# A decoder layer with routed experts on one core: the list of expert units is made in routing's last tile, and first loads and constants move with it

## What is computed

```python
logits = x_flat.astype(jnp.float32) @ gate_weight.astype(jnp.float32).T
scores = jax.nn.sigmoid(logits)
...
_, topk_idx = jax.lax.top_k(tmp, K)                      # K = 8 of E = 64 experts
...
xe = jnp.zeros((E, CAP, H), x.dtype).at[sorted_e, pos].set(tok_sorted, mode='drop')
h = jax.nn.silu(jnp.einsum('ech,efh->ecf', xe, w1)) * jnp.einsum('ech,efh->ecf', xe, w3)
ye = jnp.einsum('ecf,ehf->ech', h, w2)
...
out = jax.ops.segment_sum(vals * flat_w[:, None], flat_t, num_segments=T)
shared = jax.nn.silu(x @ shared_gate.T) * (x @ shared_up.T) @ shared_down.T
return (out + shared).reshape(B, S, H)
```

## Time and profile before

| | us |
|---|---|
| median of the timed runs (3) | 3640.21 |
| lowest, highest | 3639.7, 3642.63 |
| time of the profiled execution | 3623.67 |
| its span | 3621.7 |
| TensorE busy in the span | 3162.4 (87%) |
| VectorE, ScalarE, GpSimd busy | 2182.0, 1384.8, 1553.3 |

### The profile page before, as it was taken

The page is one execution under the profiler, slowest core; times in us unless marked ns, Lnnn a source line. Parts: engine busy times, 40 slices in busy tenths (PEclk is TensorE's granted clock), DMA queues, the critical chain, the costliest instruction groups (busy, mean ns, idle before and its releaser), DMA issues. The chain is left out here.

```text
span 3621.7 us, 63739 instructions
## 1 busy us (share of the span) xinstructions
PE 3162.4 (87%) x18589; PEld 2035.1 (56%) x18589; DVE 2182.0 (60%) x4857; ACT 1384.8 (38%) x3155; POOL 1553.3 (43%) x1113
## 2 busy tenths in 40 slices
PE   7998989999899998989796999999788882999990
PEld 4444444454444444444344777776676671888880
DVE  3645556455564645556354788886566662777775
ACT  1443434434354443434322556664000001444441
POOL 3352434424244342434531333342366664666661
PEclk8999999989999999999898999998899996999995
DMA  4122121222203122120283112121321212898996
GB/s 120 40 68 72 33 69 39 68 72 53 78 14 87 48 68 72 31 58 18 86 271 116 58 62 68 62 62 47 106 58 52 60 51 85 232 254 252 248 254 208
DMA packets 189332, 343.99 MB, mean 95 GB/s; under 512 B 36153, under 2 KB 54714, under 8 KB 188090
## 3 DMA queue, kind: packets, MB, share of 16 engines
q1 hardware_dynamic: 132922, 242.51, 23.5%
q0 software_dynamic: 28800, 48.43, 5.9%
q10 hardware_dynamic: 27392, 50.34, 3.8%
HBM read 206.96 MB, written 83.89 MB: 80 GB/s over the span
## 5 line engine op out<-in xcount | busy, mean ns | idle before, releaser
L544 ACT ACTIVATE sa_probs<-sa_s 128x512 f32<-128x512 f32 (+3 forms) x1280 | 615.0, 537 | 747.5 <-PE sa_s L435 414.8
L329 POOL TENSOR_TENSOR sa_both<-sa_probs 128x2048 f32<-128x2048 f32 (+2 forms) x160 | 589.6, 3685 | 696.0 <-PE sa_pv L462 684.5
L401 PE MATMUL sa_w<-sa_parts 96*128 96x512 f32 (+3 forms) x1280 | 518.9, 457 | 115.6 <-DVE sa_pmax L603 34.8
L435 PE MATMUL sa_s<-sa_parts 128*128 128x512 f32 (+3 forms) x1280 | 459.7, 410 | 18.9 <-ACT sa_probs L544 13.7
L607 DVE TENSOR_REDUCE sa_pmax<-sa_w 128x1 f32<-128x512 f32 (+3 forms) x768 | 419.3, 584 | 87.7 <-PE sa_w L401 84.4
L401 PEld LDWEIGHTS sa_w<-sa_parts 96*128 96x128 f32 x1280 | 238.4, 197 | 408.0 <-issue 119.8
L603 DVE CUSTOM_DVE_ANT_0 sa_w<-sa_w,sa_maskS 128x512 f32<-128x512 f32 (+3 forms) x512 | 326.3, 649 | 230.9 <-PE sa_w L401 224.5
L435 PEld LDWEIGHTS sa_s<-sa_parts 128*128 128x128 f32 x1280 | 244.5, 195 | 130.5 <-ACT sa_probs L544 64.4
L1384 POOL DMA_INDIRECT token_and_weight_of_slot<-rt_entry,rt_sl x256 | 254.7, 995 | 142.5 <-issue 74.9
L453 PE MATMUL sa_pv<-sa_probs,sa_values 128*32 128x512 f32 (+3 forms) x2560 | 275.7, 549 | 0.0
L1202 ACT ACTIVATE xa_sm<-xa_sm,xa_nmax 128x154 f32<-128x154 f32 x512 | 208.8, 410 | 64.6 <-DVE xa_nmax L1146 64.6
(11 more groups left out here) (240 smaller groups left out, 5786.5 us busy)
## 6 DMA issues: line engine op xcount, KB each, us to landing
ex_w<-in_w SPq DMA_DIRECT2D x138, 512.0 KB
sa_parts<-sa_halves SPq DMA_DIRECT2D x384, 128.0 KB, 2.5
sa_xt<-in_xT SPq DMA_DIRECT2D x32, 1024.0 KB
scratch_attention_T<-sa_oT SPq DMA_DIRECT2D x32, 256.0 KB, 2.2
on_at<-scratch_attention_T SPq DMA_DIRECT2D x32, 256.0 KB, 3.3
on_xr<-in_x SPq DMA_DIRECT2D x32, 256.0 KB, 3.3
scratch_x<-on_xn ACTq DMA_DIRECT2D x32, 256.0 KB, 2.1
scratch_x_T<-on_xnT ACTq DMA_DIRECT2D x32, 256.0 KB, 3.3
```

The costliest lines, as they stand in the source:

```text
L329: pool.tensor_tensor(both[:, :, 0:w], probs[:, even, :, 0:w], probs[:, odd, :, 0:w], ALU.add).then_inc(both_ready, 1)
L401: nc.tensor.matmul(ps[:, 0:w], qparts[0:3 * HD, h, q0:q0 + P], kparts[0:3 * HD, h, k0:k0 + w], start=True, stop=True).then_inc(work_ready, 1)
L435: mm = nc.tensor.matmul(ps[:, 0:w], kparts[:, h, kb * P:(kb + 1) * P], qparts[:, h, q0:q0 + w], start=True, stop=not diag)
L544: nc.scalar.activation(probs[:, r % NPB, h, 0:w], sbank[n % NSB][:, 0:w], ACT.Exp).then_inc(exp_done, 1)
```

## The change

A class `Lists` holds what both stages use: the list, the table's copy in SBUF (`entries`), the matrix for transposes, a zero column, both buffers of the experts' weights, and the semaphores of their loads and of `added`. The second block of routing goes. Its parts and the experts' head are moved:

- GpSimd: the three constants of the list stand at routing's head, ahead of `consts`; behind it the experts' four constant steps and the four stores into `unused`.
- TensorE: the sum over `cum` behind the last tile, into `gps` (with two waits that are met by then).
- VectorE: `list_units` in the last tile's `locate`, behind the reciprocal and ahead of the wait for GpSimd's product.
- SyncE, behind its last tile: the list goes from SBUF to SBUF instead of by DRAM; it reads the first unit and loads its weights; then it waits for all scatters and loads the table. The first load in `experts` is gone.
- `experts` has no wait for constants any more; its loop is the same.

```diff
@@ route_and_shared
+                sp.wait_ge(worklist_done, 1)
+                sp.wait_ge(lists.set_up, 1)
+                sp.dma_start(lists.worklist[0:1, 0:2 * UNITS].rearrange("o (u c) -> o u c", c=2), wli[:]).then_inc(lists.worklist_in, 16)
+                sp.wait_ge(lists.worklist_in, 16)
+                first = sp.value_load(lists.worklist[0:1, 0:1], min_val=0, max_val=UNITS - 1) // UPE
+                lists.load_weights(sp, first, 0)
+                for s in range(2):
+                    sp.wait_ge(scat[s], 128 * (NT // 2))
+                sp.dma_start(lists.entries[:].rearrange("p n e c -> p n (e c)"),
+                             table.rearrange("(n p e) c -> p n (e c)", p=P, e=E_)).then_inc(lists.entries_in, 16)
...
+                step(pool.iota(iou[:], pattern=[[1, UNITS]], base=0, channel_multiplier=0))
+                step(pool.iota(row[:], pattern=[[0, 1]], base=1, channel_multiplier=1))
+                step(pool.memset(zrow[:], 0.0))
                 pool.sem_inc(consts, 1)
+                step(pool.memset(lists.worklist[:], 0))
+                step(pool.memset(lists.zero[:], 0.0))
+                step(pool.memset(lists.identf[:], 0.0))
+                step(pool.affine_select(out=lists.identf[:], in_=lists.identf[:], compare_op=ALU.not_equal, fill=1.0, base=0,
+                                        pattern=[[-1, P]], channel_multiplier=1))
+                pool.sem_inc(lists.set_up, 1)
+                for n in range(2 * J):
+                    pool.dma_start(unused[n], lists.zero[:]).then_inc(lists.added, 16)
...
                 each_tile(pe, body)
+                pe.wait_ge(cum_done, NT)
+                pe.wait_ge(sc_done, NT)
+                nc.tensor.matmul(gps[:, 0:E_], ones[:], cum[:, NT % 2], start=True, stop=True).then_inc(tot_done, 1)
...
                     step(dve.reciprocal(wrec[:], wrec[:]))
+                    if isinstance(t, int) and t == NT - 1:
+                        list_units()
                     dve.wait_ge(oh_done, t + 1)
...
-        with nc.Block() as block:
-            @block.gpsimd
-            def _(pool):
-                pool.iota(iou[:], pattern=[[1, UNITS]], base=0, channel_multiplier=0).then_inc(lconst, 1)
...
-            @block.sync
-            def _(sp):
-                sp.wait_ge(tot_done, 2)
-                sp.dma_start(worklist, wli[:]).then_inc(wl_out, 16)
-                sp.wait_ge(wl_out, 16)
@@ experts
-            sp.dma_start(entries[:].rearrange("p n e c -> p n (e c)"), table.rearrange("(n p e) c -> p n (e c)", p=P, e=E_)).then_inc(entries_in, 16)
-            sp.wait_ge(consts, 1)
-            sp.dma_start(wl[:, 0:2 * UNITS], worklist.rearrange("u c -> (u c)").unsqueeze(0)).then_inc(wl_in, 16)
...
-            each_unit(sp, lambda: load(0, 0), lambda w, s: load(w + 1, 1 - s))
+            each_unit(sp, lambda: None, lambda w, s: load(w + 1, 1 - s))
...
-            for n in range(2 * J):
-                pool.dma_start(unused[n], zero[:]).then_inc(added, 16)
             pool.wait_ge(added, 2 * J * 16)
             pool.wait_ge(listed, 2)
```

More of the change, by code:

```diff
@@ L1268, with __init__, sb, load_weights @@
 SPARE = UNIT
-def route_and_shared(nc, sems, x2, x2T, gateT, ebias, sgT, suT, sdT, res, table, worklist):
+AHEAD = 2
+COLS = CAP // P
+J = UNIT // P
+class Lists:
+    def __init__(self, nc, ctx, w1T, w3T, w2T):
+        def sb(name, shape, dt=F32):
+            return ctx.enter_context(nc.sbuf_tensor("list_" + name, shape, dt))
+        self.w1T, self.w3T, self.w2T = w1T, w3T, w2T
+        self.worklist = sb("worklist", [1, 2 * (UNITS + AHEAD)], I32)
+        self.entries = sb("entries", [P, COLS, E_, 2])
+        self.identf = sb("identf", [P, P])
+        self.zero = sb("zero", [P, 1])
+        self.w1 = sb("w1", [P, 2, KT, FF])
+        self.w3 = sb("w3", [P, 2, KT, FF])
+        self.w2 = sb("w2", [P, 2, FF // P, DM])
+        self.set_up = kept_semaphore(nc, ctx, "list_set_up")
+        self.worklist_in = kept_semaphore(nc, ctx, "list_worklist_in")
+        self.entries_in = kept_semaphore(nc, ctx, "list_entries_in")
+        self.w_in = [kept_semaphore(nc, ctx, f"list_w_in{i}") for i in range(2)]
+        self.added = kept_semaphore(nc, ctx, "list_added")
+    def load_weights(self, sp, e, s):
+        for dst, src in ((self.w1, self.w1T), (self.w3, self.w3T), (self.w2, self.w2T)):
+            sp.dma_start(dst[:, s], src[e]).then_inc(self.w_in[s], 16)
+def route_and_shared(nc, sems, x2, x2T, gateT, ebias, sgT, suT, sdT, res, table, unused, lists):
     with ExitStack() as ctx:
@@ L1621, in experts @@
-def experts(nc, sems, x2, table, worklist, w1T, w3T, w2T, res, unused):
-    J = UNIT // P
+def experts(nc, sems, x2, lists, res):
     FT = FF // P
@@ L1645, in experts @@
         sig = sb("sig", [P, FT * UNIT]); hg = sb("hg", [P, FT * UNIT]); hT = sb("hT", [P, FT * UNIT]); hTh = sb("hTh", [P, 2, 2, FT, UNIT], F32R)
[L1646 removed]
+        y = sb("y", [P, 2, J, DM])
         tps = [ps(f"tps{i}") for i in range(2)]; h1 = [ps(f"h1{i}") for i in range(1)]; h3 = [ps(f"h3{i}") for i in range(1)]
         yps = [ps(f"yps{i}") for i in range(2)]
[L1649 to L1651 removed]
+        wl_in, entries_in, w_in, added = lists.worklist_in, lists.entries_in, lists.w_in, lists.added
+        w_high = sem("w_high"); w_low_v = sem("w_low_v"); w2_low = sem("w2_low")
+        listed = sem("listed")
         source_set = sem("source_set"); target_set = sem("target_set"); factor_set = sem("factor_set")
@@ L1656, in experts @@
         sig_done = sem("sig_done"); hg_done = sem("hg_done"); h_done = sem("h_done"); h_high = sem("h_high"); h_low = sem("h_low")
[L1657 removed]
+        y_done = sem("y_done")
         block = ctx.enter_context(nc.Block())
@@ L1773, in _ @@
             pe.sem_inc(g2_done, 2)
-            pe.wait_ge(consts, 1)
             def turn(w, s):
@@ L1822, in _ @@
             act.sem_inc(sig_done, 1)
-            act.wait_ge(consts, 1)
             def split_high(w, s, n):
@@ L2010, in program @@
                         t["c_bv"], t["c_bo"], x1, x1T, x2, x2T)
-        route_and_shared(nc, sems, x2, x2T, t["gate"], t["e_bias"], t["s_gate"], t["s_up"], t["s_down"], res, table,
-                         worklist)
-        experts(nc, sems, x2, table, worklist, t["w1"], t["w3"], t["w2"], res, unused)
+        with ExitStack() as kept_lists:
+            lists = Lists(nc, kept_lists, t["w1"], t["w3"], t["w2"])
+            route_and_shared(nc, sems, x2, x2T, t["gate"], t["e_bias"], t["s_gate"], t["s_up"], t["s_down"], res, table, unused, lists)
+            experts(nc, sems, x2, lists, res)
         last_norm(nc, sems, res, t["out"])
```

88 lines of the change are left out of this document (29 added, 59 removed).

## The result

The changed kernel took 3616.26 us (median of 3 runs, 3612.07 to 3619.21) against 3640.21: ratio 0.9931, 95% interval 0.9909 to 0.9954, so 16.7 to 33.1 us faster, 24.0 by the medians. A repetition of both kernels, with 9 runs against 30, gave 3587.42 against 3602.67 us: ratio 0.9955, interval 0.9941 to 0.9969, 16.2 us. A third, with 6 against 11, gave 0.9953 (0.9936 to 0.9970), about 17 us. The forecast was 19.1 us and 3621.1. What follows takes the time apart by stretches, because the size of the gain in the traces is 15.7 us at the place that the forecast spoke of, and not 24.

The account below looks back on a forecast made before the run. TensorE bounds the experts' loop (437.23 of 470.50 us); the seam waits for GpSimd, barriers and DMA. Profiled 3623.67 us less the seam's 19.1 gives 3604.6; with 16.5 carried over, 3621.1 us, range 3614 to 3629.

Parts of the forecast that it names:

- the seam: Between routing and experts: first expert matmul at 3050.4 instead of 3069.5, a gain of 19.1 us.
- The list and its cover: Last routing tile: VectorE's 2.98 us list chain hides under its 8.49 us wait for GpSimd's product, cost 0.
- T: Experts' first instruction: 1.55 us after the unchanged barrier at 3035.3, so at 3036.8, 7.25 us earlier.
- The copy: GpSimd's first copy at the experts' start: near T+2.5, dearer by 0.97 us beside VectorE's splits.
- The landing of the gather: First unit's gather, sharing DMA with unit 1's weights: landed at T+9.2.
- upper bound: First gather's landing if both gathers and unit 1's weights share DMA evenly: 2.6 MB in 6.4 us, T+10.4.
- Landing to first matmul: From first gather landed to first expert matmul: stays 4.36 us, TensorE at its 1.2 GHz level.
- The head of routing: Constants and stores moved to routing's start hide under TensorE's idle time: cost 0, upper bound 0.7 us.
- The loop: Experts' 45 units: work untouched, units still 10.4 to 10.5 us apart.
- The slower rhythm: Rival in the experts' loop: adds and weight loads meet in another phase; 0.6 us a unit gives 3648; chance 0.04.
- the larger gain: Rival: unit 0 runs faster with early successor weights and GpSimd's drain shrinks; up to 23 us, 3617; chance 0.08.
- The 16.5 us: Whole kernel: timed median 3640.21 lies 16.5 us above the profiled execution; carried over to the forecast without a cause.

Follow-up runs that it names:

- e_gather_alone: Changed kernel plus one wait: SyncE holds the weights of units 1 and 2 until the first gather has landed; 3617.74 us, ratio to before 0.9948.
- e_stores_back: Changed kernel with the four stores into `unused` issued at the experts' head again; 3595.95 us, ratio to before 0.9978.
- e_list_back: Changed kernel with the list, first weights and table's load in a block of their own behind the last scatters; 3601.28 us, ratio to before 0.9990.
- e_stores_early: Kernel before with only the four stores into `unused` moved to routing's head; 3601.77 us, ratio to before 0.9996.
- r_after2: Changed kernel run again without edits, on a third chip with long routing; 3617.47 us, ratio to before 0.9953.
- r_before: Kernel before run again without edits, for a second trace; 3600.48 us.
- e_two_units: Changed kernel with both first units' weights loaded in routing's tail, a wait for the first gather, loads two units ahead; 3617.64 us, ratio to before 0.9948.

## Why the prediction was right, and where it was not

**The sign, the place and the two mechanisms** were right, the size of the seam was not, and how near the median came is luck. The seam shrank by 15.7 us (38.55 to 22.82, means of four traces each), by what was named: one barrier block less, and the completion of the stores off the path.

**The list and its cover: as forecast.** Cost 0, under the wait that shrank from 8.49 to 5.18 us. The Trainium skill (GPSIMD Engine Reference, section 1, Specifications) has GpSimd's SBUF interface contended by VectorE instructions with two SBUF inputs. The trace shows no cost of it here: the scatters beside the list kept 0.98 us. That holds for the list alone; elsewhere in routing single scatters took up to 1.48 us, in both kernels, and no run tells why. The weights were issued 14 us ahead of the last scatter's end, where 13 was forecast (3018 against 3031).

**T, the experts' first instruction.** Forecast 5.73 us behind the last scatter, measured 5.9 to 6.2: 0.2 to 0.5 us missed. The barrier opens as before, at the end of GpSimd's drain of 2.68 us, 4.2 us behind the scatter's end (3040.11 to 3044.3).

**The copy** was forecast at T+2.5 and came at T+2.36. It got dearer by 0.26 us (0.44 instead of 0.18), not by the 0.97 of the loop.

**The landing of the gather is the term that was mis-sized:** T+9.2 in the sum, T+10.4 as its upper bound, and T+12.2 in the trace (3046.32 to 3058.50). The bound counted only 2.6 MB: two gathers and unit 1's weights. In the trace SyncE issues unit 1's three loads from 3048.1 (T+1.8) and three more from 3051.6: unit 2's weights (into unit 0's buffers) may go as soon as unit 0 is split, and with early weights that is early too. That makes 3.1 MB of weights and 1.05 MB of gathers, 4.2 MB. Of these 3.5 MB had moved when the first gather was there, and the engines were busy until 3060. The rows of before held the answer: there too six loads stood beside the gather, and it was landed 10.2 us behind the first of them. e_gather_alone, which takes all those weights away, gives T+8.7, and a seam of 18.98 where 19.3 (38.45 less 19.1) was forecast. That it meets the forecast is in part luck: the forecast counted on unit 1's weights beside the gather, and put a gather without weights at T+7.7, because its 1.8 us from the last issue to the landing were 2.64. How far unit 1's weights alone would delay the gather no run shows; with both units' it is 3.5 us (T+8.7 to T+12.2). The question to ask was which gate of SyncE the early split opens next.

**Landing to first matmul:** 4.36 forecast, 4.37 measured, at a granted clock of 0.50, the 1.2 GHz level, in every stretch from 3048 to 3062, after 41 idle microseconds of TensorE.

**The head of routing: cost 0, as forecast**, by the first gate matmul, +11.0 us in both kernels on one chip. But tiles in the middle of routing are 1.9 us longer in sum with the change (427 against 425), a cost that no step of the forecast has. e_stores_back has 425.0 and e_list_back 426.9 there, so it comes and goes with the stores' place in the changed kernel; e_stores_early, with early stores in the kernel before, has 425.5. TensorE's waits for ScalarE's `rt_sc` go with it: 37.1 to 37.2 us in the three traces at 427, 26.8 to 30.6 in the four at 425, and 34.0 in e_stores_early. Why the stores' place changes them stays open.

**The loop: unchanged**, 486.9 to 487.4 us against 487.1 to 487.9. The slower rhythm did not come, nor did the larger gain.

**The 16.5 us** between the profiled execution and the median, carried over without a cause, were wrong as a constant: in the changed kernel the profiled execution is one of the three timed ones and is their median, 3616.26. What varied between traces was routing: 488.1 us in the trace of before, 500.7 in that of after, 499.7 to 504.9 in four traces of changed kernels on the chip of r_after2. Carried to the profiled execution of after, the forecast (3604.6) is 11.7 us too low: 12.5 of routing and 3.4 of the seam, less 3.5 from a routing that began earlier (2539.5 against 2542.9), less 0.5 from the experts' part and the norm and less 0.2 in what the time has over the span. By the medians the seam's 15.7 us alone would have given 3624.5, above the forecast. The measured median lies another 8.3 us lower, and neither the traces nor the repetitions (16.2 and 17 us) give these. That the two misses leave only 4.8 us between median and forecast is luck.

**Whose the gain is**, by seams: the stores 7.1 us taken alone and 9.2 put back; everything but the stores 6.6, of which the first weights are nothing, so this is the list's block and what stood around it. 6.6 and 9.2 are the two steps from before over e_stores_back to after, so their sum is the whole by its making and proves nothing. The shares depend on the order: the stores taken alone and everything else alone make 13.7 us, 2.1 less than both together.

## What to carry to other kernels

A load that is moved earlier opens the gates of the loads behind it, so count what will be on the DMA engines at the new time, up to the transfer that is waited for, and hold back what is not yet needed: one wait on SyncE gave 3.7 us here, and loads made even earlier gave nothing. A small store whose completion only sets a semaphore costs its full latency where engines wait for it (6 to 8 us here), and belongs ahead of them by more than that. Repeat both kernels on another chip before a difference between timed gain and traced gain is explained by the change.

## What the runs showed of the hardware

- Four stores of one word a row: from the end of the last issue to the release of the waiting engine 6.3 us in the kernel before and 7.7 us in e_stores_back, with DMA at 0 to 1 GB/s. From issue to landing it was 6.5 us in r_before and 8.8 us at routing's head in e_stores_early (medians of the four). The list of 1 KB, SBUF to SBUF, released SyncE's reading in 1.9 us (3023.07 to 3025.0).
- A gather of two issues lands 2.6 us behind its last issue alone (e_gather_alone, e_two_units), and 5.2 to 6.8 us behind it beside weight loads, in the other twelve traces.
- GpSimd's drain at the end of routing takes 2.68 us in all fourteen traces.
- Routing takes 470 to 473 us on two chips and 488 to 505 on a third and in the first two profiles, there with gaps of up to 1.2 us in TensorE's queue that have no releaser in the profile.
